# Mean and variance from rounded parts and rests, one output product behind V, and a subtraction moved from GpSimd to VectorE

## The reference, cut to what matters

```python
def attn_layer(x, Wqkv, qs, ksc, Wo):
    qkv = x @ Wqkv
    ...
    q = l2norm(q) * qs
    k = l2norm(k) * ksc
    ...
    q = q * cos * scale + rotate_half(q) * sin * scale
    ...
    out = local_attention(q, k, v)     # 16 heads of 64, windows of 32 tokens
    return out @ Wo

def ffn_layer(x, g, bln, W1, b1, W2, b2):
    mu = x.mean(-1, keepdims=True)
    var = ((x - mu) ** 2).mean(-1, keepdims=True)
    xn = (x - mu) / jnp.sqrt(var + 1e-05) * g + bln
    hg = xn @ W1 + b1
    a, gate = jnp.split(hg, 2, -1)
    return a * jax.nn.gelu(gate, approximate=False) @ W2 + b2
```

## Time and profile before

| what | value |
|---|---|
| median of 3 runs | 1649.42 us (1645.71 to 1653.0) |
| the profiled execution, its own time | 1650.14 us |
| its span in the profile | 1648.3 us |
| PE, PEld busy | 1562.5 us (95%), 1280.8 us (78%) |
| DVE, ACT, POOL busy | 1305.7 us (79%), 1280.5 us (78%), 1202.1 us (73%) |
| mean granted clock of TensorE | 0.98 |

### The profile page before, as it was taken

How to read it: one execution, slowest core, us unless ns; L and a number is a source line. 1 busy time by engine, 2 the same in 40 slices (tenths; PEclk the granted TensorE clock), 3 DMA queues, 4 the chain that set the end, 5 groups by cost and what they waited for, 6 DMA issues and landing times.

```text
span 1648.3 us, 90156 instructions
## 1 busy us (share of the span) xinstructions
PE 1562.5 (95%) x37082; PEld 1280.8 (78%) x37082; DVE 1305.7 (79%) x1944; ACT 1280.5 (78%) x2012; POOL 1202.1 (73%) x906
## 2 busy tenths in 40 slices
PE   7898699999999999999999999999999999999977
PEld 3575578888888888888888888888888888888865
DVE  5475868888888888888888888888888888888863
ACT  5696557788787888887888878788787788887863
POOL 2201757879878879878779788789788788787741
PEclk9798799999999999999999999999999999999998
DMA  3000223332324322334233333332342223322221
GB/s 128 2 0 1 50 64 103 72 71 64 86 66 121 71 53 70 93 73 110 59 72 71 83 106 73 75 71 52 93 117 71 65 60 88 79 63 67 69 64 40
DMA packets 75729, 116.75 MB, mean 71 GB/s; under 512 B 17294, under 2 KB 27276, under 8 KB 74764
## 3 DMA queue, kind: packets, MB, share of 16 engines
q1 hardware_dynamic: 75660, 115.99, 28.3%
HBM read 19.04 MB, written 1.05 MB: 12 GB/s over the span
## 4 chain that ended last, share of the span: by engine, by line
PE 93%; issue 4%; DVE 1%; ACT 1%; POOL 0%; DMA 0%; SPq 0%; ACTq 0%; DVEq 0%; POOLq 0%
PE ps L681 17%; PE ps L947 10%; PE ps L922 9%; PE ps L873 9%; PE ps L798 9%; PE ps L801 8%; PE ps L802 8%; PE ps L866 3%; PE ps L963 3%; PE ps L670 2%; PE ps L965 2%; PE ps L964 2%; PE ps L958 1%; PE ps L954 1%; PE ps L702 1%
## 5 line engine op out<-in xcount | busy, mean ns | idle before, releaser
L456 POOL TENSOR_TENSOR arena<-arena 128x1024 f32<-128x1024 f32 x192 | 457.4, 2382 | 68.7 <-DVE arena L1630 55.1
L465 POOL TENSOR_TENSOR arena<-arena,rnorm 128x1024 f32<-128x1024 f32 x192 | 361.7, 1905 | 86.6 <-ACT rnorm L1236 86.6
L681 PE MATMUL ps<-cst,arena 64*128 64x64 f32 x6656 | 290.3, 230 | 36.8 <-issue 15.2
L681 PEld LDWEIGHTS ps<-cst,arena 64*128 64x128 f32 x6656 | 249.8, 140 | 87.6 <-issue 74.1
L1225 ACT ACTIVATE arena<-ps 128x1024 f32<-128x1024 f32 x192 | 197.0, 1026 | 104.9 <-DVE arena L1630 98.0
L1626 DVE TENSOR_TENSOR arena<-ps,rope 128x1024 f32<-128x1024 f32 x192 | 233.8, 1218 | 31.2 <-PE ps L802 28.5
L1630 DVE TENSOR_TENSOR arena<-ps,rope 128x1024 f32<-128x1024 f32 x192 | 233.3, 1215 | 0.0
L801 PE MATMUL ps<-wqkv_lo,x_hi 128*128 128x512 f32 x576 | 228.3, 396 | 0.0
L802 PE MATMUL ps<-wqkv_hi,x_hi 128*128 128x512 f32 x576 | 227.9, 396 | 0.0
L1640 DVE TENSOR_REDUCE norm<-arena 128x16 f32<-128x1024 f32 x192 | 224.5, 1209 | 0.3 <-ACT arena L1225 0.2
L798 PE MATMUL ps<-wqkv_hi,x_lo 128*128 128x512 f32 x576 | 200.6, 430 | 0.6 <-issue 0.6
(11 more groups left out here) (153 smaller groups left out, 2933.8 us busy)
## 6 DMA issues: line engine op xcount, KB each, us to landing
v_sb<-v_nat SPq DMA_DIRECT2D x576, 130.0 KB
v_sb<-v_nat SPq DMA_DIRECT2D x192, 65.0 KB
wqkv_sb<-wqkv SPq DMA_DIRECT2D x6, 1536.0 KB, 6.2
v_sb<-v_sb SPq DMA_DIRECT2D x96, 65.0 KB
wo_sb<-wo SPq DMA_DIRECT2D x6, 512.0 KB, 3.7
w_sb<-w SPq DMA_DIRECT2D x6, 341.0 KB, 4.0
x<-xT SPq DMA_DIRECT2D x1, 1024.0 KB, 5.2
scl<-scales SPq DMA_DIRECT2D x6, 128.0 KB, 6.0
```

What stands on the lines that cost most here:

```text
L456: pool.tensor_tensor(t_cos[:, m, j, :], t_cos[:, m, j, :], t_sin[:, j, :], ALU.add)\
L465: pool.tensor_tensor(x, x, rnorm[:, H * j:H * j + H].unsqueeze(2).to_broadcast([P, H, D]), ALU.mult).then_inc(s[done], 1)
L681: mm = pe.transpose(ps[0:width, bank + t, 64 * c:64 * c + 64], src[r], ident[r, r], tile_position=(64 * t, 0))
```

## The change

Five things are done.

1. **Mean and variance.** GpSimd rounds the 128x256 operand into `f_nh` (fp32r) and subtracts it from the operand into `f_nl`, once for the shifted input (`part_x`) and once for the squares (`part_square`). TensorE multiplies both by a matrix `mean_r` of 1/128 (exact in fp32r), so that one fp32 product becomes two fp32r products (`mean_of_parts`). In the tail the fp32 products stay.
2. **Order on ScalarE.** `square(g-2)` stands before `copy_q(g,1)`, where it stood after `copy_p(g,0)`.
3. **Output.** `project_out(g-1)` does seven products, then comes v of `g+1`, then the eighth.
4. **The rest of x.** `low` moves from GpSimd to VectorE: `low(g+1,1)` in front of the first norms, `low(g+2,0)` at the slot's end.
5. **Room.** Constants that only the start reads (`cst_first`) lie in the arena, in a DMA of their own; `a_vs` moves; GpSimd stages it after `a_roped`; two more memsets; one more cast on VectorE.

The diff, cut to its core:

```diff
-        cst = sb("cst", [P, C_END])
+        cst = sb("cst", [P, C_KEPT])
...
+        f_nh = sb("f_nh", [P, N], F32R)
+        f_nl = sb("f_nl", [P, N], F32R)
+        mean_r = sb("mean_r", [P, P], F32R)
...
-            def low(pair, m):
-                n = 2 * pair + m
-                col = (pair & (B - 1)) * HP + P * m
-                pool.wait_ge(s["x_high"], CREDIT + 2 * n + 2)
-                pool.tensor_tensor(x_lo[0:64, m, :], h0[0:64, bass.ds(col + 1, P)],
-                                   x_hi[0:64, m, :].bitcast(F32), ALU.subtract).then_inc(s["x_split"], 1)
-                pool.wait_ge(s["x_split"], CREDIT + 2 * n + 1)
-                pool.tensor_tensor(x_lo[64:128, m, :], h0[64:128, bass.ds(col, P)],
-                                   x_hi[64:128, m, :].bitcast(F32), ALU.subtract).then_inc(s["x_split"], 1)
...
+            def part_x(f):
+                pool.wait_ge(s["f_shifted"], CREDIT + 2 * f + 2)
+                pool.wait_ge(s["f_var"], CREDIT + f)
+                pool.sem_inc(s["pool_waited"], 1)
+                pool.tensor_copy(f_nh[:, :], f_x).then_inc(s["f_x_rounded"], 1)
+                pool.wait_ge(s["f_x_rounded"], CREDIT + f + 1)
+                pool.tensor_tensor(f_nl[:, :], f_x, f_nh[:, :].bitcast(F32), ALU.subtract)\
+                    .then_inc(s["f_x_parted"], 1)
+
+            def part_square(f):
+                pool.wait_ge(s["f_squared"], CREDIT + f + 1)
+                pool.wait_ge(s["f_mean"], CREDIT + f + 1)
...
                 scale(g, 1)
+                if norm:
+                    part_x(f)
                 if ahead:
                     rotate(g + 1, 0, 0)
-                    low(g + 1, 1)
                     rotate(g + 1, 0, 1)
                     if ff:
                         part_gated(g - LAG)
+                    if norm:
+                        part_square(f)
...
-                    if more:
-                        low(g + 2, 0)
...
+            def mean_of_parts(parted, f, bank, done):
+                pe.wait_ge(s[parted], CREDIT + f + 1)
+                pe.matmul(ps[:, bank, 0:N], mean_r[:, :], f_nl[:, :], start=True, stop=False)
+                pe.matmul(ps[:, bank, 0:N], mean_r[:, :], f_nh[:, :], start=False, stop=True).then_inc(s[done], 1)
...
-                        variance(g - 2, 2)
+                        mean_of_parts("f_sq_parted", g - 2, 2, "f_var")
                     if att:
-                        project_out(g - 1)
+                        project_out(g - 1, end=7)
                     if norm:
                         pe.wait_ge(s["f_log"], CREDIT + g - 1)
                     v(g + 1, 0)
+                    if att:
+                        project_out(g - 1, first=7)
...
+                if norm:
+                    square(g - 2)
                 copy_q(g, 1)
                 copy_k(g, 1)
                 copy_p(g, 0)
...
-                if norm:
-                    square(g - 2)
...
+            def low(pair, m):
+                n = 2 * pair + m
+                col = (pair & (B - 1)) * HP + P * m
+                dve.wait_ge(s["x_high"], CREDIT + 2 * n + 2)
+                dve.tensor_tensor(x_lo[0:64, m, :], h0[0:64, bass.ds(col + 1, P)],
+                                   x_hi[0:64, m, :].bitcast(F32), ALU.subtract).then_inc(s["x_split"], 1)
+                dve.tensor_tensor(x_lo[64:128, m, :], h0[64:128, bass.ds(col, P)],
+                                   x_hi[64:128, m, :].bitcast(F32), ALU.subtract).then_inc(s["x_split"], 1)
```

More of the change, by code:

```diff
@@ L58 @@
 LAST_BANKS = {SLOTS - 3: (2, 3, 1), SLOTS - 2: (5, 4, 0), SLOTS - 1: (2, 3, 1)}
-C_ID, C_MEAN, C_SUM2, C_MASK = 0, 128, 256, 384
-C_ROPE = C_MASK + 2 * SPAN
-C_ROPE1 = C_ROPE + U * 4 * D
+C_ID, C_MEAN, C_ROPE = 0, 128, 256
+C_KEPT = C_ROPE + U * 4 * D
+C_SUM2 = C_KEPT
+C_MASK = C_SUM2 + P
+C_ROPE1 = C_MASK + 2 * SPAN
 C_END = C_ROPE1 + AG * AT
@@ L189, in build @@
         a_ks = f_a1[:, 1, :].rearrange("p (k t) -> p k t", k=2)
-        a_vs = take(10496, CH).rearrange("p (k j h d) -> p k j h d", k=2, j=4, h=2)
+        cst_first = take(10496, C_END - C_KEPT)
+        sum2_w = cst_first[:, C_SUM2 - C_KEPT:][:, 0:P]
+        a_vs = take(11264, CH).rearrange("p (k j h d) -> p k j h d", k=2, j=4, h=2)
         a_p = take(0, 8, N)
@@ L433, in _ @@
             pool.memset(f_sq, 0.0).then_inc(s["zeroed"], 1)
+            pool.memset(f_nh[:, :].bitcast(F32), 0.0).then_inc(s["zeroed"], 1)
+            pool.memset(f_nl[:, :].bitcast(F32), 0.0).then_inc(s["zeroed"], 1)
             pool.memset(f_ah[:, :, :].bitcast(F32), 0.0).then_inc(s["zeroed"], 1)
@@ L503, in rest @@
                 pool.tensor_tensor(f_lo[:, :], f_y, f_hi[:, :].bitcast(F32), ALU.subtract).then_inc(s["f_split"], 1)
+            def part_x(f):
[9 more added lines that the diff above has]
+                pool.wait_ge(s["f_mean"], CREDIT + f + 1)
+                pool.sem_inc(s["pool_waited"], 1)
+                pool.tensor_copy(f_nh[:, :], f_sq).then_inc(s["f_sq_rounded"], 1)
+                pool.wait_ge(s["f_sq_rounded"], CREDIT + f + 1)
+                pool.tensor_tensor(f_nl[:, :], f_sq, f_nh[:, :].bitcast(F32), ALU.subtract)\
+                    .then_inc(s["f_sq_parted"], 1)
             def part_gated(f):
@@ L524, in split_down, with slot @@
                 part.then_inc(s["w2_ready"], B)
-            def slot(g, norm=True, ff=True, ahead=True, more=True, after=None, layer=None):
+            def slot(g, norm=True, ff=True, ahead=True, after=None, layer=None):
                 f = g - 2
                 scale(g, 1)
+                if norm:
+                    part_x(f)
                 if ahead:
                     rotate(g + 1, 0, 0)
-                    low(g + 1, 1)
                     rotate(g + 1, 0, 1)
@@ L583, in _ @@
             ln_divide_second(pool, 1)
-            low(0, 0)
-            low(0, 1)
             ln_divide_second(pool, 2)
@@ L591, in _ @@
             rotate(0, 1, 0)
-            low(1, 0)
             rotate(0, 1, 1)
@@ L609, in _ @@
                 slot(pool.snap(g))
-            slot(SLOTS - 2, more=False)
+            slot(SLOTS - 2)
             slot(SLOTS - 1, ahead=False)
@@ L1055, in slot @@
                     pe.wait_ge(s["f_gated"], CREDIT + 3 * (g - LAG) + 3)
-                    mean(g - 2, 6)
+                    mean_of_parts("f_x_parted", g - 2, 6, "f_mean")
                 if att:
@@ L1084, in slot @@
                         down_parted(g - LAG)
-            pe.wait_ge(s["zeroed"], 14)
-            pe.wait_ge(s["bf_ready"], 2)
+            pe.wait_ge(s["zeroed"], 16)
+            pe.wait_ge(s["bf_ready"], 3)
             q(0, 0)
@@ L1699, in add, with slot @@
                                          of_sequence(h1, f), ALU.add, ALU.add).then_inc(s["f_done"], 1)
-            def slot(g, att=True, norm=True, ff=True, ahead=True):
+            def slot(g, att=True, norm=True, ff=True, ahead=True, more=True):
                 if att:
@@ L1719, in slot @@
                 if ahead:
+                    low(g + 1, 1)
                     norms(g + 1, 0)
@@ L1733, in slot @@
                     norms(g + 1, 1)
+                    if more:
+                        low(g + 2, 0)
             def final(b):
@@ L1741, in _ @@
             dve.wait_ge(s["a_pv"], CREDIT + 2 * AH)
+            low(0, 0)
+            low(0, 1)
             rope_products(0, 0, 0)
@@ L1749, in _ @@
             norms(0, 1)
+            low(1, 0)
             dve.wait_ge(s["h0_ready"], B)
@@ L1754, in _ @@
             slot(2, ff=False)
-            with dve.Fori(LAG, SLOTS - 1) as g:
+            with dve.Fori(LAG, SLOTS - 2) as g:
                 slot(dve.snap(g))
+            slot(SLOTS - 2, more=False)
             g = SLOTS - 1
```

26 lines of the change are left out of this document (13 added, 13 removed).

## The result

The changed kernel took 1857.06 us (median of 4 runs, 1852.38 to 1859.05), the kernel before 1647.57 us beside it: a ratio of 1.1255, 95% interval 1.1226 to 1.1284. It is slower, as forecast, but by 209 us where the forecast said 55, and above the range's end of 1785.

A forecast was written before the change was run, and what follows sets the result against it. The prediction took TensorE, with 93% of the chain, to bound the kernel. Subtractions waiting behind GpSimd, less mean and variance savings, gave +1.2 us over 46 slots: 1650.1 + 55 = 1705 us, range 1640 to 1785.

The forecast's parts named there:

- Mean and variance, 0.38 per slot: On TensorE, two fp32r products replace one fp32 product, saving 0.19 us at each of mean and variance, 17 us in all.
- Both are hidden; I cost them at nothing: GpSimd's part_x and part_square, under 1.56 us each, were taken to fit in its idle time without delaying TensorE.
- c=0.41: VectorE's time for a pair of subtractions, taken by starts as 0.41 us; whole records gave 0.57.
- 2c-0.58: Slot change without GpSimd interference, c being the pair's time on VectorE: about +0.2 us per slot, +0.55 at c of 0.57.
- The slot's end, 0.9 to 1.4 us of VectorE: The slot-end pair waits for GpSimd's last rotation, making VectorE 0.9 to 1.4 us late and TensorE 0.5 to 1.0.
- +0.8 at (c): In the middle of a slot the pair waits 0.4 us for GpSimd's cast and takes 0.4 us itself.
- (c): The second half's turn_o on TensorE waits for VectorE's division; room at most 0.1 us, taken as none.
- Rival 2: The pair's second subtraction also waits, behind GpSimd's next operation: 1.7 us more per slot, 1781 us; chance 0.15.
- L1650 over 1.5 us: Sign of Rival 2: the subtraction on VectorE at source line L1650 takes over 1.5 us.
- My argument against it: Against Rival 2: GpSimd waits for its own cast in the middle, leaving a gap in which the pair may get through.
- +1.2 forecast: Net slowdown per slot from both pairs' waits less the mean and variance savings: summed to +1.35, taken as +1.2 us.
- (d): turn_q on TensorE waits 0.3 us behind v_copied; the split output product removes this, but the gain becomes a wait elsewhere.

The follow-up runs named there:

- e8: The kernel before with two idle reductions of 512 columns on VectorE ahead of the middle's norms: 1703.0 us.
- e15: The kernel before with three idle reductions of 512 columns on VectorE ahead of the middle's norms: 1762.7 us.
- e4: The kernel before with four idle reductions of 512 columns on VectorE ahead of the middle's norms: 1808.5 us.
- e1: The changed kernel with all subtractions of x back on GpSimd, all else as in the change: 1645.73 us, ratio to before 0.9996.
- e2: The kernel before with only the subtractions moved to VectorE: 1896.64 us.
- e5: The changed kernel with each of VectorE's two subtractions replaced by a one-input reduction of the same 64x128 elements: 1671.03 us.
- e7: The changed kernel with only the slot-end pair (and the start's pairs) on VectorE, the middle pair back on GpSimd: 1719.51 us.
- e6: The changed kernel with only the middle pair (and the start's pairs) on VectorE, the slot-end pair back on GpSimd: 1787.39 us.
- e12: The changed kernel with all subtractions back on GpSimd and the eighth output product back in front of v: 1645.62 us, ratio 0.9986.
- e10: The changed kernel with subtractions back on GpSimd, the mean in fp32 again, and turn_k ahead of the first attend: 1644.88 us, ratio 0.9982.
- e11: The changed kernel with all subtractions back on GpSimd and turn_k ahead of the first attend: 1642.84 us, ratio 0.9975.

## Why the prediction was right or wrong

- **The direction and the place: right.** VectorE's chain in front of `turn_o` decides, with no room (about 0.6 us per reduction in e8, e15 and e4); the subtractions wait for GpSimd; e1 and e2 put the whole loss there.
- **Mean and variance, 0.38 per slot: right** in six slots of eight (e1: 0.36, of which 0.06 is the split product's).
- **"Both are hidden; I cost them at nothing": wrong** in two of eight. The cover was read in a slot in which GpSimd splits no weights. Without it, e1's two long slots cost 1.35 and 1.7 us each, which ate the gain of the other six.
- **c=0.41: wrong end.** The pair takes 0.61 us by starts (e5), nearer to 0.57, the sum of the records, which the rule gives that the prediction took from the Trainium skill, "VectorE: DVE Perf Modes", section "Two Vector instructions with no wait between them". The trace agrees: e5's reductions start 0.30 apart, a whole record. The formula 2c-0.58 gives 0.56 with 0.57, against 0.51 measured; with the measured 0.61 it gives 0.64, so that this agrees so well is in part luck.
- **The slot's end, 0.9 to 1.4 us of VectorE: right in a plain slot.** In the changed kernel the pair holds VectorE there for 0.9 to 1.1 us. TensorE pays 0.64 per slot for it (e7 over e1), a little under the 0.7 to 1.2 that the sum had ahead of the mean's 0.19. The weight slots, in which a pair meets a whole rotation, were not seen.
- **The middle, "+0.8 at (c)": the step that failed.** The forecast let the pair wait behind GpSimd once; it costs 2.6 us per slot at the full clock (e6 over e1). The first subtraction waits as forecast. The second falls behind GpSimd's subtraction of 1.8 us, in 44 of 47 pairs: Rival 2's mechanism, to which I gave 0.15, and its sign, L1650 over 1.5 us, is there (1.87). My argument against it was the gap between GpSimd's cast and its subtraction. That gap is 0.08 us (1009.82 to 1009.90), and what frees the first half at the cast's end lets it finish 0.14 later, when the next operation is running. So after one wait, with GpSimd's next operation ready, the second was nearly sure.
- **The clock: a term missing.** From slot to slot: +1.2 forecast, +1.7 for the second half (Rival 2's own price), +1.4 for the clock: 4.3, against 34.04-29.79=4.25 measured. By the runs: e1's 29.43, 0.64 for the end pair, 2.6 for the middle pair and 1.4 for the clock make 34.1. The weight slots bring the mean to 4.7. Rival 2's 1781 lacked these two, the clock and the weight slots.
- **(d): right that no time comes of it, for another reason.** `turn_q` no longer waits, and that is the split output product's doing: from 500 to 1500 us it waits in 4 slots in e1, and without the split (e12) in 33, by 0.18 us. But the first `attend` now waits 0.24 us for `add`; with `turn_k` between them 0.14 to 0.18 us of it come out (e10, e11).

## What to carry to other kernels

Before moving a small VectorE operation beside a busy GpSimd, look at what GpSimd runs at that moment in every kind of slot, and count up to one full GpSimd operation for each VectorE operation of a form that was held here (a copy, a `tensor_scalar`, a `tensor_tensor` with two SBUF inputs). Two in a row are two waits where GpSimd has its next operation ready, since the first one's release is that operation's start. TensorE's pauses of 1.75 us and more had a second price here, 1.5 us at the lower clock, in many slots. Work that is hidden in the common slot must be looked at in the rare ones too.

## What the runs showed of the hardware that was not expected

- A `tensor_scalar` of 64x128 with one SBUF tensor on VectorE is held for GpSimd's operation (1.87 us) like a `tensor_tensor` with two (1.89 us); a `tensor_reduce` of the same elements at the same place never is (0.266 to 0.281 us in 96).
- The clock's loss is of one size, 1.4 to 1.55 us a slot, and its frequency differs: none of 44 slots behind pauses of 1.15 us, 19 behind 1.75, 34 behind 2.3, but about half in e6 behind 2.5 us. What decides between slots with the same pause stays open.
